# First attention: the scaling of the probabilities of units 0 and 3 of each tile, on GpSimd instead of ScalarE

## The reference

```python
def _gqa(q, k, v):
    scale = 1.0 / np.sqrt(q.shape[-1])
    scores = jnp.einsum('bsghd,btgd->bghst', q, k) * scale
    p = jax.nn.softmax(scores, axis=-1)
    return jnp.einsum('bghst,btgd->bsghd', p, v)
...
q = _ln(_fp8_linear_pertensor(ln_out, wq, wq_scale, q_in_scale).reshape(b, s, g, hpg, d), qln_w, qln_b)
k = _ln(_fp8_linear_pertensor(ln_out, wk, wk_scale, k_in_scale).reshape(b, s, g, d), kln_w, kln_b)
v = _fp8_linear_pertensor(ln_out, wv, wv_scale, v_in_scale).reshape(b, s, g, d)
core = _gqa(q, k, v).reshape(b, s, nh * d)
...
catq = _div_clamp_fp8(jnp.concatenate([core, xout], axis=-1), proj_smooth)
return jnp.einsum('bsi,oi->bso', catq, wproj) * (proj_in_scale * proj_w_scale)
```

## Time and profile before

| what | value |
|---|---|
| median of 3 runs | 1504.31 us (1501.78 to 1506.41) |
| the profiled execution: its time | 1502.7 us |
| its span | 1500.9 us |
| busy over the span | TensorE 1437.8 us (96%), VectorE 877.0 (58%), ScalarE 768.6 (51%), GpSimd 526.4 (35%) |
| probability scaling (L890) | 256 activations, 82.4 us |

### The profile page before, as it was taken

The page is one execution under the profiler, slowest core; times in us unless marked ns, Lnnn a source line. Parts: engine busy times, 40 slices in busy tenths (PEclk is TensorE's granted clock), DMA queues, the critical chain, the costliest instruction groups (busy, mean ns, idle before and its releaser), DMA issues. The chain is left out here.

```text
span 1500.9 us, 22370 instructions
## 1 busy us (share of the span) xinstructions
PE 1437.8 (96%) x7006; PEld 1040.2 (69%) x7006; DVE 877.0 (58%) x1923; ACT 768.6 (51%) x2123; POOL 526.4 (35%) x522
## 2 busy tenths in 40 slices
PE   6999999999989999999999999999997999999998
PEld 5677777788875555557878888866764666665656
DVE  5798988899875242333464545455677555553322
ACT  5888888999982211110234444444357655553210
POOL 2767677877761000000533333322111333321000
PEclk9999999999999999999999999999999999999999
DMA  5301000200006511112100000000232000011120
GB/s 204 118 6 64 5 5 1 97 1 1 2 1 265 180 53 49 49 50 91 67 1 1 0 1 1 15 15 6 102 150 97 1 1 1 1 30 43 47 69 17
DMA packets 21880, 71.67 MB, mean 48 GB/s; under 512 B 3922, under 2 KB 6354, under 8 KB 19076
## 3 DMA queue, kind: packets, MB, share of 16 engines
q1 hardware_dynamic: 13556, 57.38, 10.4%
q10 hardware_dynamic: 8208, 12.87, 2.8%
HBM read 69.01 MB, written 1.22 MB: 47 GB/s over the span
## 5 line engine op out<-in xcount | busy, mean ns | idle before, releaser
L1282 ACT ACTIVATE l0f_silu<-bank 128x512 f32<-128x512 f32 x48 | 28.5, 597 | 198.9 <-PE bank L1206 183.0
L948 POOL TENSOR_TENSOR l0a_head_rstd<-l0a_head_var,all_minus_half 128x4 f32<-128x4 f32 x96 | 99.6, 1042 | 18.2 <-DVE l0a_head_var L666 18.2
L1385 DVE TENSOR_TENSOR l0f_product<-l0f_silu,bank 128x512 f32<-128x512 f32 x48 | 32.9, 687 | 124.3 <-ACT l0f_silu L1282 124.2
L920 POOL TENSOR_TENSOR l0a_stepped<-l0a_y,l0a_m 128x512 f32<-128x512 bf16 x64 | 73.8, 1153 | 89.1 <-DVE l0a_m L644 87.5
L484 PEld LDWEIGHTS bank<-l0a_k_t,l0a_q_t 128*128 128x128 f32 x512 | 63.7, 191 | 39.7 <-ACT l0a_q_t L832 35.3
L846 ACT ACTIVATE l0a_work<-bank,l0a_neg_max 128x128 f32<-128x128 f32 x256 | 90.3, 372 | 1.2 <-DVE l0a_neg_max L679 1.2
L1218 PEld LDWEIGHTS bank<-all_weights_a,l0f_hidden 128*128 128x128 f32 x384 | 72.9, 190 | 25.3 <-issue 17.0
L1814 DVE TENSOR_TENSOR all_weights_a<-bank,all_cols 128x512 f32<-128x512 f32 x64 | 43.9, 690 | 77.6 <-PE bank L1649 46.2
L1218 PE MATMUL bank<-all_weights_a,l0f_hidden 128*128 128x256 f32 x384 | 88.9, 379 | 0.0
L2407 PE MATMUL bank<-l3a_f_xn_t,all_weights_b 128*128 128x512 f32 x192 | 86.2, 594 | 0.0
L890 ACT ACTIVATE l0a_work<-l0a_work,l0a_row_inv 128x128 f32<-128x128 f32 x256 | 82.4, 411 | 6.2 <-DVE l0a_row_inv L683 5.9
(11 more groups left out here) (443 smaller groups left out, 3760.3 us busy)
## 6 DMA issues: line engine op xcount, KB each, us to landing
l0f_spread<-l0f_weights ACTq DMA_DIRECT2D x32, 192.0 KB, 2.7
all_weights_a<-in_l_w_q SPq DMA_DIRECT2D x2, 2048.0 KB, 13.8
l0f_spread<-l0f_weights ACTq DMA_DIRECT2D x32, 128.0 KB, 2.8
all_weights_b<-in_l_e_gate_up SPq DMA_DIRECT2D x1, 3200.0 KB, 10.4
all_weights_b<-in_l_e_gate SPq DMA_DIRECT2D x1, 3072.0 KB, 10.0
all_weights_a<-in_l_e_up SPq DMA_DIRECT2D x4, 768.0 KB, 6.7
all_weights_a<-in_l_e_down SPq DMA_DIRECT2D x1, 3072.0 KB, 15.2
l3a_spread<-l3f_weights SPq DMA_DIRECT2D x10, 256.0 KB, 3.4
```

The lines of the kernel that those rows point to most:

```text
L920: done = g.tensor_tensor(stepped[:, 0:n], value, step, ALU.add)
L948: g.tensor_tensor(head_rstd[:, m % 2, :], head_var[:, m % 2, :], res.minus_half[:, 0:HU], ALU.pow)\
```

## The change

`scale_probs` is split by query unit. For units 0 and 3 (`POOL_SCALED`) GpSimd does one `tensor_tensor` over 128 x 512, with the four reciprocals broadcast along each head, instead of ScalarE's four activations over 128 x 128. It stands in GpSimd's list at the same steps "query + 6": unit 3 of the tile before in step 5, and unit 0 in step 7. Units 1 and 2 stay on ScalarE, which for unit 1 also waits until GpSimd has counted unit 0. Line numbers behind the change are up to 14 higher.

```diff
--- before.py
+++ after.py
@@ -345,6 +345,7 @@
         KV_TILE, KV_CENTRE, KV_HIGH, KV_LOW = 1, [6, 14], [7, 9, 15, 17], [8, 12, 16, 22]
         Q_TILE, Q_CENTRE = 4, [6, 8, 14, 22]
         OUT_LOW = list(range(8))
+        POOL_SCALED = (0, 3)
         OUT_FIRST_HIGH, OUT_FIRST_LOW = [2, 4, 6, 8], list(range(3, 11))
 
         def quant_parts(b):
@@ -884,7 +885,11 @@
             act.wait_ge(affine_ready, 1)
 
             def scale_probs(b, a):
+                if a in POOL_SCALED:
+                    return
                 inv_ready.wait(act, inv_ready.at(b, a + 1))
+                if a - 1 in POOL_SCALED:
+                    probs_ready.wait(act, probs_ready.at(b, a))
                 for h in range(HU):
                     pr = probs[:, a % 2, h * P:(h + 1) * P]
                     done = act.activation(pr, pr, ACT.Copy, scale=row_inv[:, a, h:h + 1])
@@ -953,6 +958,14 @@
                 projected_out.wait(g, projected_out.at(b, a - 1))
                 round_to(y16[:], m16[:], cat[:, a % 2, :], BANK, mixed_taken.sem).then_inc(cat_done.sem, 1)
 
+            def scale_probs(b, a):
+                if a not in POOL_SCALED:
+                    return
+                inv_ready.wait(g, inv_ready.at(b, a + 1))
+                probs_ready.wait(g, probs_ready.at(b, a))
+                pr = heads(probs[:, a % 2, :])
+                g.tensor_tensor(pr, pr, along(row_inv[:, a, :], P), ALU.mult).then_inc(probs_ready.sem, 1)
+
             def out_low(p, a, half):
 
                 g.wait_ge(p_high, p * NA + a + 1)
@@ -973,7 +986,8 @@
                 g.tensor_tensor(f_rstd[:], f_var[:], res.minus_half[:, 0:4], ALU.pow).then_inc(f_rstd_ready, 1)
 
             quantise(-1, 0)
-            march(VTS, STEPS, [(round_mixed, later(at_query, 9)), (rstd, later(at_norm, 1)), in_tile(F_ROWS_TILE, first_rstd, F_ROWS[0:1]),
+            march(VTS, STEPS, [(round_mixed, later(at_query, 9)), (rstd, later(at_norm, 1)), (scale_probs, later(at_query, 6)),
+                               in_tile(F_ROWS_TILE, first_rstd, F_ROWS[0:1]),
                                in_tile(0, out_low_first, OUT_FIRST_LOW), (quantise, [4, 6, 8]),
                                in_tile(EARLY_TILE, quantise_early, EARLY_QUANT),
                                in_tile(LAST_X, out_low_second, later(OUT_LOW, QUERY[0] + 11))])
```

## The result

The kernel after took 1535.42 us in the median of 4 runs (1532.93 to 1537.7), the kernel before on the same chip 1504.43 (4 runs, 1501.78 to 1506.41): 31.0 us more, ratio 1.021, 95% interval 1.0189 to 1.023. The forecast was 1529, 24.9 us more. The profiled execution took 1535.73 us, its span 1534.0, which is 33.1 more than before.

The account below looks back on a forecast made before the run. Bound: TensorE in the first pass; in the second a GpSimd-VectorE loop close to TensorE's own. Second pass 13.2, first 7.7, tile 8 2, ends 2, ScalarE's relief 0: 24.9 us more, median 1529 us, range 1516 to 1551.

Parts of the forecast that it names:

- The loop of the second pass: Closed loop through GpSimd, VectorE and TensorE in a second-pass tile: 27.3 us against 25.1, at most 29.8.
- (c): Second pass, GpSimd: rounding unit 1, rstd, input part, scaling unit 3, to next rounding: 6.29 us, 6.9 with VectorE's split delayed.
- (d): Second pass, GpSimd: rounding unit 2, rstd, input part, scaling unit 0, until its transposes can start: 6.22 us.
- the last lap: Second pass, from rounding unit 0 to rounding unit 1 of the next tile, all GpSimd-VectorE ping-pong: 6.06 us.
- (a): Second pass, from unit 0's transposes to rounding the next unit 0: 8.1 us if VectorE catches up, upper bound 10.39.
- that rival: VectorE doesn't catch up while TensorE stands, in both passes: 49 us more, 1553 us; chance 0.12.
- The sum of the second pass: Added time of the six tiles with three input parts, 9 to 14, at 2.2 us each: 13.2 us.
- The first pass: Tiles 1 to 7, loop closing through TensorE: 26.5 to 27.9 us against 25.73, taken as 1.1 more each, 7.7 us.
- The hold-up: VectorE's bf16 split beside GpSimd's new operation, in the second pass, ends 0 to 0.85 us later, taken as 0.6.
- The rival without a hold-up: GpSimd's new operation doesn't delay VectorE's bf16 operations, else as forecast: 21 us more, 1526 us; chance 0.15.
- the rival in which ScalarE was what TensorE waited for: At scores and transposes, scaling never late, so all 8.7 us of TensorE's waits go: 1496 us; chance 0.05.
- The rival in which the scaling fits into GpSimd's gaps: GpSimd's idle time before roundings takes the scaling, the old ping-pong stays: 1508 us, no change; chance 0.07.

Follow-up runs that it names:

- e1_unit3: Changed kernel with only unit 3's scaling on GpSimd, unit 0's back on ScalarE: 1534.93 us, 31.6 more than the kernel before.
- e5_filler: Changed kernel plus twelve identity transposes on TensorE ahead of its wait for unit 3's probabilities in the second pass: 1533.18 us, 29.0 more than the kernel before.
- e9_load_wide: Kernel before plus, at the scaling's places, a GpSimd 128 x 512 operation on its own buffer, nobody waiting, no drains: 1520.32 us, 16.3 more.
- e2_unit0: Changed kernel with only unit 0's scaling on GpSimd, unit 3's back on ScalarE: 1525.09 us, 21.7 more than the kernel before.
- e7_unit3_filler: Only unit 3 on GpSimd, plus twelve identity transposes ahead of TensorE's second-pass wait for unit 3: 1523.78 us, 19.6 more than the kernel before.
- e6_relief: Kernel before, ScalarE scaling only one column of one head for units 0 and 3, the rest left unscaled: 1503.03 us against 1504.18.
- e10_load_narrow: Kernel before plus, at the scaling's places, a GpSimd power of 128 x 4 for which nobody waits: 1504.79 us, 0.8 more.
- e4_ahead: Changed kernel with GpSimd's scaling one step earlier, between rstd and the input part's rounding: 1519.33 us, 16.0 more than the kernel before.

## Why the prediction was right, and where its sizes were off

**The loop of the second pass** came out at the forecast number, 27.36 us against 27.3, in part by luck. GpSimd's pieces are as forecast: in the tile from 319.75 (c) is 6.81 us (forecast 6.9, with the hold-up), (d) from 326.56 to the end of the scaling at 332.74 is 6.18 (6.22), the last lap 6.06. But the loop doesn't close there. TensorE comes to unit 0's transposes 0.26 us behind GpSimd, since it ran at half clock behind the wait for unit 3, and e1_unit3 has the same 27.4 us with no second scaling at all. Where the clock is kept (e5_filler) the forecast's loop is the one that closes, with the wait on unit 0 that I had named, and it gives 26.94 us in tiles 10 and 12: (c) 6.82, (d) 6.18, (a) 7.76 instead of 8.1, 6.18. So the forecast was some 0.4 us too long for its own path, and the clock, which it left out, filled the place. VectorE did catch up, so that rival falls: from the transposes at 333.00 to the rounding of unit 0 it is 8.05 us, not 10.39.

**The sum of the second pass** was 13.2 and is 15.6 us. Five of the six tiles cost 2.26 to 2.50, since their base was 24.89 to 25.10 and, for the last, 25.78; tile 9, the first with three input parts, cost 3.44. TensorE's clock has a part in that: e5_filler takes 1.4 us off this tile, against 0 to 0.8 off the five.

**The first pass** was right in its mechanism and the term most off in its size: 7.7 forecast, 12.1 measured. Four of seven tiles cost 1.0 to 1.35 us, near the 1.1, and the tile of 26.90 us stands beside the forecast 26.8. There the loop closes as forecast, through TensorE at clock 1.00: from the rounding at 201.70 6.09 us to the end of unit 3's scaling (6.13), 0.05 to its transposes, 6.30 to unit 0's (6.24), 8.40 to the rounding of unit 0 (8.1 to 9.42), 6.06. Tiles 3 and 5 cost 2.9 each and tile 7 1.75. I had one tile stand for all. In tile 3 input parts are quantised early and stand in GpSimd's program ahead of unit 0's scaling: with unit 0 alone the tile has 2.1 of its excess, with unit 3 alone 1.0. In tile 5 unit 3 alone gives 2.8: there VectorE's weight preparation and the half clock behind the wait of 2.28 us fall together; which of the two weighs how much no run here separates. I had also left the hold-up of VectorE out of the first pass; the load alone costs 5.2 us over these seven tiles in e9_load_wide, but in the changed kernel L641 is held up beside a scaling in three of them only (1, 5 and 7), and what it costs there is not shown apart.

**The clock** was no term of the sum. The front matter gave 1.00 for the stage before, and I never asked what a wait of 2 to 4 us would do to it. In the changed kernel nine stretches at 0.50, of 3 us and more, stand in the first attention, each beginning in or just behind a wait for L967; before there was none. In the second-pass tiles the path with the half clock is about as long as GpSimd's loop, which is why the forecast could hold without it; with one unit moved nothing else is as long and the clock shows in full, 1.3 to 1.4 us a tile, which is most of what my expectations for e1_unit3 and e2_unit0 missed in the second pass. The fillers show it for both. The Trainium skill has the rule (TensorE: Matmul & The Clock Gate, Part 1): the half rate is where the array stands by default and activity releases it. The traces here agree, 0.50 behind waits and 1.00 with filler in the same place. But not every such wait brings it: in e2_unit0 a wait of 2.33 us that ended at 127.32 and one of 2.39 us that ended at 407.25 were followed by 1.00, one of 2.39 us that ended at 379.48 by 0.50.

**The hold-up** was counted in one lap only, at 0.6 us. It is 0.68 us where L641 meets the wide operation, so the size was right, and in the changed kernel's second pass it is in that one lap, as forecast. But since TensorE's path sets the tile there, it is not on the path that closes: with the clock kept and unit 3 alone (e7_unit3_filler, tile 10) 6.16 us to the end of the scaling, 0.05, 5.71 on TensorE, 8.06 and 6.06 make the 26.04 without it. Where nobody waits for the added operation it meets both places of a tile and sets the pace: 16.3 us of load without any dependence, of which the narrow operation of the same length shows only 0.8 to be GpSimd's time. I counted L641 on the mixed output beside the wide operation and above 0.45 us: 18 of 64 in e9_load_wide, 12.1 us longer together, and 11 of 64 in the changed kernel, 7.7 us longer. L641 on the mixed output has a mean of 423 ns in the changed kernel, with 315 ns for L640 before, as the prediction named it. By the Trainium skill (SBUF — State Buffer, "Who interferes with whom") whoever of the two issues first holds the shared port pair for the whole instruction. The trace agrees to within what it shows: L641 issued 0.26 to 0.27 us into the wide operation and ended 0.14 to 0.15 us behind it, in both passes and in e9_load_wide. The rival without a hold-up falls: (c) would be 6.3.

**TensorE's waits** came where they were named on unit 3 (2.1 to 2.3 us in tiles 10 to 14, up to 3.8 in tiles 8 and 9, 0.8 to 2.3 in the first pass; 31.9 us in 18 times over the stage; forecast lateness 2.1 and 3.2). On unit 0 in tiles 10 to 14 they did not come, since TensorE at half clock is later than GpSimd by then; with the clock kept they came, 1.1 us in tile 10 (e5_filler).

**ScalarE's relief** at 0 is shown by e6_relief, so the rival in which ScalarE was what TensorE waited for falls. Its busy time fell by 35.1 us and not by 52.6. I had multiplied 128 activations by the mean of 411 ns, but by the same row 256 of them were busy only 82.4 us, since they overlap: half of that is 41. The other 6 us stay open. (A misread row without weight: TensorE was busy 25.73 of 25.73 us in the first-pass tile of the earlier trace rows, not 25.71.)

**The other terms**: tile 8 cost 3.0 (forecast 2), the first tile and the tail together 3.3 (2), the later layers gave 0.9 back. With 15.6 and 12.1 these are the 33.1 us of the span; the two medians differ by 31.0, and the forecast of 24.9 was for either.

**The gaps.** The rival in which the scaling fits into GpSimd's gaps falls with the tiles, though e10_load_narrow shows that it was right about the queue where nobody waits: 32 operations of the same length do fit in. It was not GpSimd's busy time that ran short.

The 31 us are not a sum of one part for each mechanism. The load alone costs 16.3 us (e9_load_wide), TensorE's wait with the clock kept and unit 3 alone 26.0 instead of 25.1 us in tile 10, the half clock another 1.3 in it, and unit 0's scaling 0 to 0.9 according to the clock. In each tile the longest path decides, and the others lie beside it. What the runs show as a difference is this: the same operations one step earlier give 15.0 us back (e4_ahead), and the clock kept in tiles 9 to 15 gives 2.0 us back with both units moved and 12.0 with unit 3 alone.

## What to carry to other kernels

Moving work to an engine with gaps is judged by the closed loop that runs through it, and by what stands in its queue ahead of the moved step: here the receiving engine was 77% busy and the price was still 2%. A wide GpSimd operation can cost its neighbour too: look at which of VectorE's 16-bit operations will run beside it, since a wide and a narrow operation of equal length differed by 15.5 us here. And where a change makes TensorE wait for 2 us and more, look at the granted clock behind the wait, in every tile. A tile time that comes out as forecast doesn't show that the forecast's loop closes: remove one term of it, as e1_unit3 does, and see whether the time moves.

## What the runs showed that I had not expected

- One GpSimd operation on 128 x 512 f32 of 1.09 us, for which nobody waits, cost 16.3 us over 32 times, 0.5 us each; a power on 128 x 4 of 1.06 us, as often, cost 0.8 us.
- Behind most single waits of TensorE of 2.1 to 2.6 us in the second pass the granted clock was 0.50 for some 3 us, of which TensorE was busy all 3 in the tile shown; 12 or 14 transposes of the identity inside the wait kept it at 1.00 and gave 12.0 and 8.1 us back with one unit moved.
- Moving unit 3 alone cost as much as moving two units, 31.6 and 31.0 us: behind its wait TensorE at half clock hides what unit 0's scaling would add in the second pass.
